# Expert dispatch of a two-layer decoder: who normalises the last groups, who stores the pads, and when the first weights are loaded

## What is computed

```python
xt = layernorm(x)                          # (4096, 128)
probs = softmax(xt @ Wg)                   # 8 experts
topk_p, topk_i = top_k(probs, 2)           # each token picks two
topk_p = topk_p / topk_p.sum(-1)
h  = gelu(xt @ W1[e] + b1[e])              # second mixture: silu(x@gate) * (x@up)
eo = h @ W2[e] + b2[e]
x  = x + sum over its two experts of topk_p * eo
```

## Time and profile before

| | us |
|---|---|
| median of 3 runs (lowest, highest) | 1555.7 (1547.37, 1558.65) |
| profiled execution, its own time | 1560.02 |
| its span, first to last instruction | 1558.2 |
| X0: POOL's last 18 scatters, first start to last start | 773.49 to 795.50 |
| X0: PE starts on block 1 of the experts | 804.20 |
| X1: the same 18 scatters | 1383.92 to 1405.93 |
| X1: PE starts on block 1 | 1414.19 |

### The profile page before, as it was taken

How to read it: one execution, slowest core, us unless ns; L and a number is a source line. 1 busy time by engine, 2 the same in 40 slices (tenths; PEclk the granted TensorE clock), 3 DMA queues, 4 the chain that set the end, 5 groups by cost and what they waited for, 6 DMA issues and landing times. The chain is left out here.

```text
span 1558.2 us, 31374 instructions
## 1 busy us (share of the span) xinstructions
PE 1203.3 (77%) x11216; PEld 931.3 (60%) x11216; DVE 1029.1 (66%) x2332; ACT 910.8 (58%) x1721; POOL 814.5 (52%) x654
## 2 busy tenths in 40 slices
PE   6779879889777588888539994599975999837992
PEld 2556666666666356666539993266652666626992
DVE  2999999999999656887511113477644799742444
ACT  3778868878875167776225554277743766513443
POOL 1987887887785421556645552211002246674662
PEclk9899999999999678988569997699996999957996
DMA  5203203202200230011157775300004001127885
GB/s 185 89 28 111 83 28 110 84 28 110 83 28 1 58 56 8 29 33 35 43 177 231 223 231 169 88 9 15 16 18 114 9 26 36 44 78 206 251 244 179
DMA packets 98158, 140.10 MB, mean 90 GB/s; under 512 B 13709, under 2 KB 77242, under 8 KB 93716
## 3 DMA queue, kind: packets, MB, share of 16 engines
q1 hardware_dynamic: 86708, 120.41, 25.5%
q0 software_dynamic: 9088, 17.07, 3.2%
q10 hardware_dynamic: 2208, 0.61, 0.2%
HBM read 107.52 MB, written 28.16 MB: 87 GB/s over the span
## 5 line engine op out<-in xcount | busy, mean ns | idle before, releaser
L318 POOL TENSOR_TENSOR M_dbx<-M_u,M_b_sb 128x1024 f32<-128x1024 f32 x128 | 300.0, 2363 | 57.9 <-DVE M_h L377 57.2
L377 DVE TENSOR_TENSOR_SCAN M_h<-M_pA,M_dbx 128x512 f32<-128x512 f32 x256 | 297.4, 1200 | 5.9 <-POOL M_dbx L318 5.0
L530 ACT ACTIVATE M_pA<-M_dt,M_a_neg 128x504 f32<-128x504 f32 x256 | 174.7, 683 | 51.6 <-DVE M_h L377 47.0
L540 ACT ACTIVATE M_hc<-M_pT,M_cT 128x256 f32<-128x256 f32 x256 | 119.3, 467 | 55.1 <-PE M_pT L670 53.0
L2368 PE MATMUL X_bank<-F_xT,F_wbuf 128*128 128x256 f32 x624 | 150.4, 385 | 0.0
L670 PE MATMUL M_pT<-M_ident,M_h 128*128 128x128 f32 x512 | 83.6, 288 | 81.0 <-ACT M_hc L540 45.6
L2019 POOL DMA_INDIRECT F_slots<-F_line,F_pos x128 | 127.2, 993 | 36.0 <-issue 36.0
L686 PE MATMUL M_pY<-M_ident,M_hc 128*128 128x128 f32 x1024 | 141.0, 283 | 0.0
L670 PEld LDWEIGHTS M_pT<-M_ident,M_h 128*128 128x128 f32 x512 | 58.3, 145 | 133.2 <-DVE M_h L377 70.7
L686 PEld LDWEIGHTS M_pY<-M_ident,M_hc 128*128 128x128 f32 x1024 | 131.7, 200 | 1.2
L1615 ACT ACTIVATE X_pt_sb<-X_bank 128x512 f32<-128x512 f32 x128 | 76.4, 597 | 93.0 <-PE X_bank L1747 93.0
(11 more groups left out here) (329 smaller groups left out, 2786.3 us busy)
## 6 DMA issues: line engine op xcount, KB each, us to landing
M_b_sb<-M_rows_bc SPq DMA_DIRECT2D x32, 1024.0 KB, 4.7
F_wbuf<-in_F_wcat SPq DMA_DIRECT2D x39, 578.0 KB, 3.9
F_wbuf<-in_F_wcat SPq DMA_DIRECT2D x39, 450.0 KB, 4.0
X_s_sb<-F_slots SPq DMA_DIRECT2D x39, 132.0 KB, 3.8
F_xblk<-F_slots SPq DMA_DIRECT2D x39, 132.0 KB, 3.9
F_line<-F_line SPq DMA_DIRECT2D x16, 256.0 KB, 2.7
X_kT<-F_answers SPq DMA_DIRECT2D x8, 512.0 KB, 5.6
X_kv<-in_ctxT SPq DMA_DIRECT2D x2, 1344.0 KB, 10.1
```

Source lines behind the costliest of these rows:

```text
L318: pool.tensor_tensor(dbx[:, k % DBXS, :, :], u[:, g % 2, :, :], bc(b_sb[:, n, :], 1, 2), ALU.mult).then_inc(dbx_ready, 1)
L377: v.tensor_tensor_scan(h[:, k % STATES, half, :], pA[:, (2 * k + half) % DECAYS, :, :].rearrange("p b t -> p (b t)"), dbx[:, k % DBXS, hal ...
L530: act.activation(pA[:, (2 * k + half) % DECAYS, :, 1:SEQ], dt[:, g % 2, half, :].rearrange("p (b t) -> p b t", t=SEQ)[:, :, 1:SEQ], ACT.Ex ...
L540: act.activation(hc[:, k % SCALED, t, :], pT[:, 0, t, :], ACT.Identity, scale=cT[:, g % 2, t, n:n + 1]).then_inc(hc_ready, 1)
```

## The change

Four things are edited, in both X phases.

- `pool_normal` no longer normalises groups 6 and 7. VectorE does, in the new `vector_normal`, called behind `place` of the group before (steps 33 and 37); POOL keeps the reciprocal root and the copy of the token numbers.
- From step 32 on POOL issues its two scatters of the step in front of `pool_normal`, not behind it.
- The 8 pad DMAs move from SP to ACT's queue (`scalar_pads`), behind the two exponentials and ahead of the expert stage.
- SP loads the weights of blocks 0 to 4 as soon as the table is there, reads the first three row numbers, waits for pads and scatters, and then issues the rows of blocks 0 to 7 together. From block 5 on weights come as before, and from block 8 on each with its rows.

```diff
     def sync_rows(sp):
...
-        sp.wait_ge(tail_ready, 1)
-        for e in range(E):
-            t = sp.value_load(tail[0:1, e:e + 1], min_val=0, max_val=E * CAP - BLOCK)
-            sp.dma_start(slots[bass.ds(t, BLOCK), :].rearrange("(p s) c -> p s c", s=SUBS),
-                         pad[:, :, :]).then_inc(pads_in, 16)
+    def scalar_pads(act):
+        act.wait_ge(tail_ready, 1)
         for e in range(E):
+            t = act.value_load(tail[0:1, e:e + 1], min_val=0, max_val=E * CAP - BLOCK)
+            act.dma_start(slots[bass.ds(t, BLOCK), :].rearrange("(p s) c -> p s c", s=SUBS),
+                          pad[:, :, :]).then_inc(pads_in, 16)
...
+        if g < GROUPS - 2:
+            normal(pool, g)
+    def normal(eng, g):
         for t in range(TILES):
+            ins = eng.tensor_scalar(line[:, g % RING, 0, t, 0:D], xg(g)[:, t, :], ln.mean[:, t:t + 1],
+                                    ln.rstd[:, t:t + 1], ALU.subtract, ALU.mult)
         ins.then_inc(xn_ready, 1)
+    def vector_normal(v, g):
+        v.wait_ge(rstd_ready, g + 1)
+        reach(v, scattered[g % RING], 16 * 2 * TILES * (g // RING))
+        normal(v, g)
...
+        sp.wait_ge(d.table_ready, 1)
+        for j in range(WBUFS):
+            weights(j)
+        ahead = [first_row(j) for j in range(3)]
+        d.rows_written(sp)
+        for j in range(XBUFS):
+            block_rows(j, ahead[j] if j < 3 else first_row(j))
+        for j in range(WBUFS, BLOCKS):
+            weights(j)
+            if j >= XBUFS:
+                block_rows(j, first_row(j))
...
+                if i >= STEPS and in_range(g):
+                    d.pool_scatter(pool, g, n)
                 if s == 1:
                     if in_range(c - 2):
                         d.pool_normal(pool, c - 2)
...
+                    if GROUPS - 2 <= c - 2 < GROUPS:
+                        d.vector_normal(v, c - 2)
...
             d.scalar_exp(act)
+            d.scalar_pads(act)
             f.scalar_blocks(act)
```

More of the change, by code:

```diff
@@ L1967, in sync_rows @@
             sp.dma_start(line[:, g % RING, 1, :, 0:D], line[:, g % RING, 0, :, 0:D]).then_inc(twin_in[g % RING], 16)
-        sp.wait_ge(tail_ready, 1)
+    st.sync_rows = sync_rows
+    def scalar_pads(act):
+        act.wait_ge(tail_ready, 1)
         for e in range(E):
-            t = sp.value_load(tail[0:1, e:e + 1], min_val=0, max_val=E * CAP - BLOCK)
-            sp.dma_start(slots[bass.ds(t, BLOCK), :].rearrange("(p s) c -> p s c", s=SUBS),
-                         pad[:, :, :]).then_inc(pads_in, 16)
-    st.sync_rows = sync_rows
+            t = act.value_load(tail[0:1, e:e + 1], min_val=0, max_val=E * CAP - BLOCK)
+            act.dma_start(slots[bass.ds(t, BLOCK), :].rearrange("(p s) c -> p s c", s=SUBS),
+                          pad[:, :, :]).then_inc(pads_in, 16)
+    st.scalar_pads = scalar_pads
     def rows_written(sp):
@@ L2001, in pool_normal @@
                          ids[:, g, :, :]).then_inc(id_ready, 1)
+        if g < GROUPS - 2:
+            normal(pool, g)
+    st.pool_normal = pool_normal
+    def normal(eng, g):
         for t in range(TILES):
-            ins = pool.tensor_scalar(line[:, g % RING, 0, t, 0:D], xg(g)[:, t, :], ln.mean[:, t:t + 1],
-                                     ln.rstd[:, t:t + 1], ALU.subtract, ALU.mult)
+            ins = eng.tensor_scalar(line[:, g % RING, 0, t, 0:D], xg(g)[:, t, :], ln.mean[:, t:t + 1],
+                                    ln.rstd[:, t:t + 1], ALU.subtract, ALU.mult)
         ins.then_inc(xn_ready, 1)
-    st.pool_normal = pool_normal
+    def vector_normal(v, g):
+        v.wait_ge(rstd_ready, g + 1)
+        reach(v, scattered[g % RING], 16 * 2 * TILES * (g // RING))
+        normal(v, g)
+    st.vector_normal = vector_normal
     def pool_scatter(pool, g, n):
@@ L2233, in sync_blocks, with weights @@
     def sync_blocks(sp):
-        sp.wait_ge(d.table_ready, 1)
-        for j in range(BLOCKS):
+        def weights(j):
             e = sp.value_load(d.table[0:1, 1, j:j + 1], min_val=0, max_val=E - 1)
-            r = sp.value_load(d.table[0:1, 0, j:j + 1], min_val=0, max_val=E * CAP // P)
             if j >= WBUFS:
@@ L2242, in sync_blocks, with first_row, block_rows @@
                              "p e c -> p (e c)")).then_inc(wblk_in[j % WBUFS], 16)
-            if j == 0:
-                d.rows_written(sp)
+        def first_row(j):
+            return sp.value_load(d.table[0:1, 0, j:j + 1], min_val=0, max_val=E * CAP // P)
+        def block_rows(j, r):
             if j >= XBUFS:
@@ L2478, in _ @@
                     a.pool_add_bias(pool, c - 1)
+                g, n = (i - 14) // PER, (i - 14) % PER
+                if i >= STEPS and in_range(g):
+                    d.pool_scatter(pool, g, n)
                 if s == 1:
@@ L2483, in _ @@
                         a.pool_rstd(pool, c + 2)
-                g, n = (i - 14) // PER, (i - 14) % PER
-                if i >= 14 and in_range(g):
+                if 14 <= i < STEPS and in_range(g):
                     d.pool_scatter(pool, g, n)
```

## The result

The changed kernel took 1549.93 us (median of 20 executions, 1536.92 to 1555.83), the kernel before 1556.74 (20, 1547.37 to 1562.3). The ratio is 0.9943, 95% interval 0.9924 to 0.9963: 6 to 12 us faster, by less than 1%. That is the forecast's direction and the case that it held likeliest (within 1%, 0.59), but less of a gain than its 13.5 us, and 0.9 us above the upper end of the range, 1549. (The kernel before was 1.0 us slower here than the 1555.7 that the range was worked out from, so as a ratio the result lies just inside.) The profiled execution took 1551.11 us with a span of 1549.2, at a mean granted clock of 0.891 (before: 1558.2 at 0.888).

What follows compares the result with a forecast made beforehand. POOL's scatters, then SP and PE up to PE's start on block 1, were taken as the bound. Gains of 6.2 (X0) and 7.3 us (X1) sum to 13.5, from the median 1555.7 to 1542.2 us; range 1533 to 1549.

Steps and rivals of the forecast that it cites:

- POOL's part: POOL's tiles and scatters for groups 6 and 7: last scatter starts 6.2 us earlier in X0, 6.9 in X1.
- the new wait on POOL: Ahead of group 7's root, POOL waits for its statistics: some 2 to 2.7 us come back.
- its two terms: POOL's run loses tiles of two groups, 3.13 us each, and two scatters moved into idle time, 2.6 us.
- X1's statistics of group 7: On VectorE in X1, they come 1.2 us earlier, since PE no longer waits that long for POOL.
- rows may go 2.58 us after the last scatter: On SP, scatters' landing releases the first rows of blocks 2.58 us after the last scatter starts, at 791.9 and 1401.6.
- the burst: Early weights, pads and scatters, 3.98 MB in X0, 3.32 in X1, delay block 1's rows; PE starts 6.2 and 7.3 us earlier.
- my second rival: The burst delays semaphores too, so rows go only once it is written: gains 4.8 and 6.0 us, 1545; chance 0.13.
- Pads and weights: Issue costs: pads on ACT 1.17 to 1.6 us each, hidden at 1.17; five weights on SP 1.17 us each.
- A burst without effect: Rival: early weights don't delay block 1's rows, so PE gains 9.7 and 10.0 us, 1536; chance 0.27.
- A slow drain: Rival: the burst drains at 210 GB/s, X0 gains nothing and X1 3.6 us, 1552; chance 0.14, shared with gain traded away.
- Pads at 2.5 us or more: Rival: ACT's pads, over 2.5 us each (X1 2.6), land last and slow the kernel; 1576 at 4 us; chance 0.04.
- My signs of being wrong: PE's start on block 1 moves under 4 us in both phases, or new PE waits lengthen the expert stage.

Runs made afterwards that it cites:

- e9: Changed kernel with two weights loaded early and the tiles of groups 6 and 7 back on POOL; ratio 0.9989 to the kernel before.
- e10: Changed kernel with two weights loaded early and POOL's two scatters of a step behind the roots again; ratio 0.9916 to the kernel before.
- e6: Changed kernel with two weights loaded early instead of five; median 1539.87 us, ratio 0.9886 to the kernel before.
- e7: Changed kernel with pads and block loading as before, so only VectorE's tiles and POOL's early scatters; ratio 0.9898 to the kernel before.
- e12: Changed kernel with its pads on SP again, ahead of the five weights; ratio 0.9961 to the kernel before.
- e5: The whole changed kernel again, unedited, on another chip; median 1537.95 us against 1558.42 for the kernel before, ratio 0.9898.
- e8: Changed kernel with one weights load early instead of five; ratio 0.9873 to the kernel before.
- e11: Changed kernel with three weights loaded early instead of five; ratio 0.9908 to the kernel before.
- e1: Changed kernel with pads and block loading as before, on a chip with slow queue instructions; ratio 0.9928 to the kernel before.
- e4: Kernel before with only the new block loading, five early weights and rows together; ratio 1.0106 to the kernel before.

## Why the prediction was right, and where it was not

**POOL's part: right, within 1.4 us.** Tiles on VectorE took 1.11 us for 1.10; the new wait on POOL in X0 was 2.57 us for some 2.7; sixteen scatters, and the two early ones fit the idle. The last scatter starts 5.5 us earlier in X0 for 6.2 (the gap behind the copy is 0.65 us, had 0.18) and 8.3 in X1 for 6.9. Experiments e9 and e10 give its two terms by themselves.
**A term that I undersized: X1's statistics of group 7.** I passed on only the 1.20 us of PE's wait; they came 2.9 us earlier (12.07 for 14.96), and POOL's predicted wait of 2.2 us was absent. PE turned group 6 1.27 us earlier, and in this execution ran what follows faster. Timeline of PE in X1, before:

```profile
1370.22 1.84 PE L2146 MATMUL X_bank<-F_wr,F_xnT 128*128 128x8 f32 x8 [0.73 <-ACT F_xnT L2121]
1372.57 1.12 PE L1774 MATMUL X_bank<-X_ident,X_on 128*128 128x128 f32 x4 [0.51 <-DVE F_lgs L2044]
1374.37 2.08 PE L1782 MATMUL X_bank<-X_wo,X_oT 128*128 128x128 f32 x8 [0.69 <-ACT X_oT L1620]
```

and after:

```profile
1365.07 1.03 PE L2162 MATMUL X_bank<-F_wr,F_xnT 128*128 128x8 f32 x8 [0.73 <-ACT F_xnT L2137]
1366.61 0.66 PE L1774 MATMUL X_bank<-X_ident,X_on 128*128 128x128 f32 x4 [0.51 <-DVE F_lgs L2060]
1367.95 1.34 PE L1782 MATMUL X_bank<-X_wo,X_oT 128*128 128x128 f32 x8 [0.69 <-ACT X_oT L1620]
```

The same matmuls take 0.81, 0.46 and 0.74 us less: before, the granted clock was 0.50 (1.2 GHz) in all three rows; after, it was 1.00 (2.4 GHz) in the first two and fell within the third. Between the two roots its mean rose from 0.70 to 0.84. That PE's idle of 1.20 us had lowered it is not shown: e9 has that idle as well, and its first two rows take 1.03 and 0.66 us as here, while e6, e7, e10 and e12 have no idle, and theirs take 1.03, 1.11 and 2.08, so that group 7's root comes 12.7 us after group 6's and not 12.07. The 1.3 us of PE's earlier turn are the edit's; the other 1.6 are the clock's in these two profiles, and at least 0.6 of them come and go between executions.

**The step that failed: "rows may go 2.58 us after the last scatter".** I kept that distance of the kernel before, put the release at 791.9 and 1401.6 at the latest, and let only the rows themselves queue behind the burst (the five weight loads with the pads and scatters in flight beside them), landing 4 to 5 us after issue. The burst was sized rightly (3.98 MB at 302 GB/s forecast, 4.0 at 315 measured in X0; 3.32 MB forecast and 13.0 us x 261 GB/s = 3.4 in X1). But it acts one step earlier: the scatters and pads issued into it land in up to 6.6 and 9.1 us, SP waits for them, and the rows leave with it drained and land in 2.3 us. So the release came 4.5 and 4.7 us later behind the last scatter than I had put it, and the way from there to the hidden layer was 2 to 3 us shorter: two errors of opposite sign in one sum. That is my second rival, put at 0.13: 10.8 us (4.8 and 6.0) against 9.9 (3.7 and 6.2). The sign that I named for it, rows more than 3.5 us behind the last scatter, is there with 7.1 and 7.3. In e5 the two errors and an earlier last scatter cancel: its hidden layers stand 5.6 and 7.7 us below the one profile of the kernel before, 13.4 in sum, and that this is my 13.5 is luck.

The dose confirms it, in one execution each: with one, two, three and five loads early, rows go 3.1, 4.1, 4.9 and 6.8 us behind the last scatter in X0 (e8, e6, e11, e5), 2.6, 3.7, 4.5 and 5.7 in X1; e7 gets 4.8 from a single load at the wrong moment; e10 gets 2.6 from two loads at a harmless one. With two loads it is the lead that counts: issued 5.6, 6.2 and 8.1 us ahead of the last scatter (e6, e9, e10, X0), they leave the rows 4.1, 3.6 and 2.6 us behind it. The argument that I held against the rival, scatters of answers landing in 3.4 us, compares with about one load in flight (one is issued for each block there), not five. The rule that I cited (the Trainium skill, DMA: Bandwidth & Descriptors, section Queues, rings and completion order) pointed the right way, and these traces agree with it: the last scatter's landing in up to 6.6 us, for 2.3 before. I should have given it more.

What stays open is how: whether the semaphore's increment alone stands behind the weights' writes, as that rule has it, or the small packets of scatters and pads share each DMA engine's time with those of weights. Both make a landing late until the burst is through, and no run separates them.

**Pads and weights: right in cost.** Pads on ACT are 1.07 us apart in X0 and 1.19 in X1 (7 steps from 778.9 to 786.4 and from 1384.0 to 1392.3), the lower end of 1.17 to 1.6. But hidden they are not: the last pad lands last of all, 0.3 and 1.0 us behind the last scatter by SP's waits, because it too lies in the burst. (At 1.6 us a pad my own terms would have held the rows by 1.6 and 1.5 us, not 1.7.)

**Rivals that fell.** A burst without effect would have the rows land in 2.3 us, which they do, and be issued 2.58 us behind the last scatter, which they are not. A slow drain: 315 GB/s is no slow drain. Pads at 2.5 us or more: 1.1 on this chip; on the chip of e1 to e4 2.2, just under my point.

**My signs of being wrong.** The first, a move of PE's start on block 1 by less than 4 us in both phases, is absent: it moved by 3.7 and 6.2 us against group 6's root, 5.3 and 10 in the whole program. The second asked whether the expert stage gets longer, by waits that PE did not have: X1's is 1.6 us longer in the profile, of which a wait for rows explains 0.5, and 0.5 shorter in e5 (113.5), with no wait at all. I had also written that this stage is not reordered, which the early weights and rows contradict.

**Why the total is further off than the stages.** 13.5 forecast, 9.9 in the two stages, 6.8 between medians of 20 (the ratio gives 8.9, interval 6 to 12). On the chip of e5 the same kernel gained 20.5 between medians (by the ratio 15.9, interval 11 to 21; at equal clock 10.3 ± 2.2), of which the two stages have 13.4. What lies between 9.9 and 6.8 here, and between 13.4 and 20.5 there, is in the other stretches and in the clock; no run takes it apart.

**A version that may be better** is e6, two loads early. The hidden layer starts 4.2 us before e5's in the two phases together; times at equal clock show 2.5 ± 2.2; plain medians show 1.9 the other way, and the ratios (0.9886 and 0.9898) don't tell them apart, nor from e7 and e8. So it is not shown to be faster.

## What to carry to other kernels

A transfer that is moved ahead of a wait delays whatever that wait is for, if the awaited transfer is issued while the moved one is in flight: issue early no more than drains before the last awaited transfer starts, and check it by the landing times of the awaited ones. Cost an early load on three counts: its issue on the queue (e4, e12), its drain, and the landings that lie in it. Where matmuls stand in a chain, look at their granted clock before taking their time from one profile: the same order of work brought group 7's root 12.07 us after group 6's in some executions and 12.7 in others.

## What the runs showed of the hardware

- **The spread of a kernel's times goes with its clock.** In the 20 executions of the changed kernel the mean granted clock lay between 0.887 and 0.903 and the times fell with it (correlation -0.96), 11.6 us for each 0.01; on the chips of e5 and e9 9.3 and 9.1 us, on that of e1 12.7. At equal clock the scatter left is 1.6 to 2.7 us (standard deviation), so that a gain of 5 us can be seen where plain medians hardly tell 10. Changed kernels also ran at a higher mean clock than the one before (0.898 for 0.891 on e5's chip), but how much of that is an effect of the edits was not tested, so the equal-clock column is no full account of the gain.
- **A chip with slow queue instructions.** On that of e1 to e4, queue instructions near the pads took up to 0.70 us each where they take 0.02 to 0.27 elsewhere (the rows shown under e1), on SP and on ACT alike, and the kernel before took 1635.64 us for 1556 to 1558 on the other chips. Its lower mean clock (0.870 for 0.891) would account for 27 of the 77 us at 12.7 us for each 0.01; the rest is open.
- **A transfer in flight delays the landing of those issued behind it on other queues.** Scatters that land in 2.3 us alone took up to 6.8 us beside five weight loads (e5), 4.5 beside one issued at the same moment (e7), and 2.3 again once the loads had landed (e10).
- **A DMA whose address is read at run time costs the same on either queue.** Reading a number and issuing a pad takes 1.1 to 1.2 us on ACT as on SP, for all that a plain issue took 0.71 on ACT and 0.38 on SP.
